# Scores of the slot attention: 56 moving columns in place of 96

## The chip, the cores and the metric

The kernel runs on one core of a Trainium2 chip. The time is the device time of one execution in microseconds (us), from repeated runs; a profile of one execution, taken beside them, gives the trace.

## What is computed

The reference is a two-layer block on 16 sequences (batches) of 56 tokens of width 128, each with a context of 1500 rows. In order: a masked cross attention, a feed-forward with 16 experts, a **slot attention** with a gated recurrent unit (GRU), and a feed-forward with 32 experts and a capacity of 68 tokens each. The change lies in the slot attention:

```python
for _ in range(3):
    sn = rmsnorm(slots, slot_norm_w)
    q_proj = sn @ Wq.T
    scores = jnp.einsum('bkd,bmd->bkm', q_proj, k_proj) * SCALE
    attn = jax.nn.softmax(scores, axis=-2)          # over the 56 slots
    attn = attn / (jnp.sum(attn, axis=-1, keepdims=True) + EPS)
    updates = jnp.einsum('bkm,bmd->bkd', attn, v_proj)
    slots = gru_cell(updates, slots, gru_wih, gru_whh, gru_bih, gru_bhh)
```

The slots are the 56 token rows of a batch, so a batch has 56 query columns against 1500 keys. All matrices are fp32.

## The kernel before

Everything is written by hand: every engine has its own list of instructions in a fixed order, and semaphores (`wait_ge`, `then_inc`) tie them together. No planner moves anything.

**Tiling of the slot attention.** The 1500 keys of a batch are 12 chunks of 125 (`CP`, `CC`). Keys stand twice in SBUF: `keysT` (128 features x 1500, weights of the scores) and `keys` (125 keys x 129 columns per chunk, moving operand of the update, the 129th column for the sum). There is room for 8 batches (`GB`), so the 16 batches run as 2 groups. Two batches make a pair, a group has 4 pairs (`TWO`), and 3 iterations over 4 pairs are 12 **phases** per group, 24 in all. The Python function `phase` of each engine issues one phase; `phases` runs them, partly in hardware loops of four phases.

**Steps.** A phase has four **steps** (`step_of`): half of the key chunks (6, `CH`) of one of its two batches. Each step runs through the engines as follows.
- PE, `scores` (L1586 to L1600): for each of 6 chunks, two matmuls into two column strips of the array (64 and 61 key columns as weights, rows 0 to 63 and 64 to 124 of PSUM). The moving operand is the batch's queries in `qT`. The output goes to bank 2 + 2a + h, at column c*56 for chunk c. Before a step it waits for the queries, the keys and, four steps back, for ACT to have emptied the bank.
- DVE, `maxima` (L1190): the maximum over the 56 slots of each key, read from PSUM (L1197), times the key's norm (L1200).
- ACT, `exponentials` (L850): six exponentials of 56 columns (L859) from PSUM into `A`.
- DVE, `attention` (L1202): sums (L1208) and reciprocals (L1212).
- POOL, `weigh` (L696): the reciprocal times the key's norm (L702), then the shares times it (L704).
- PE, `update` (L1602), for every two steps: 12 matmuls with `A` as weights and `keys` moving (129 columns, L1611).

Steps are issued ahead: in each phase PE issues steps 3, 4, 5 and 6 counted from the phase's first, so the scores run three to six steps before their use. Between them stand the GRU of the pair of the phase before (`gru_start`, `gru_gates`: L1583 on PE, then L866, L867 and L872 on ACT, L1225 to L1242 on DVE) and the projection and queries for a later phase (`slot_proj`, `queries` on PE, L876 on ACT, L687 and L689 on POOL, L1256 and L1260 on DVE). Each engine takes its list in order.

**Loads.** The keys of the second group are loaded by SyncE (L562, L564); each load waits until the update of the last phase that uses the slot has run (L560).

**The padded columns.** A listed fp32 matmul shows as two passes, each with its weight load. In `scores` each matmul moves `WIDE` = 96 columns from `qT`, of which 56 are the batch's queries; the others are those of the second batch, or zeros. `qT` has 40 more columns per pair for it, set to zero by POOL at L671. The last 40 columns of each chunk's output fall on the place of the next chunk, which overwrites them; behind the last chunk they go to columns that nobody reads. `WIDE` serves the last feed-forward too (L1727, L1741), which the change leaves alone.

Of the kernel before, what the change touches and what calls it, by code (L numbers as in the profile page):

```python
# [15 lines left out]
B, S, D, M = 16, 56, 128, 1500  # L16
# [24 lines left out]
TWO = GB // 2  # L41
QS = 2 * S
# [7 lines left out]
WIDE = 96  # L50
# [17 lines left out]
def build_program(nc, t):  # L68

    with ExitStack() as ctx:  # L70
        def sb(name, shape, dt=F32):
            return ctx.enter_context(nc.sbuf_tensor(name, shape, dt))
# [98 lines left out]
        r1 = sb("r1", [128, NT])  # L171
# [13 lines left out]
        work = sb("work", [128, 4 * CC * S + 7 * HALF])  # L185
# [4 lines left out]
        def carve(n, where="region"):  # L190
            tile = {"region": region, "work": work, "early": early, "early_rest": early_rest}[where]
            used[where] += n
            assert used[where] <= tile.shape[1]
            return tile[:, used[where] - n:used[where]]
# [55 lines left out]
        pair_rows = ident[:, :].rearrange("p (i q) -> p i q", i=2)[:, :, 0:S]  # L250
        slots_x = carve(TWO * QS, "work").rearrange("p (a s) -> p a s", a=TWO)

        qT_all = carve(TWO * (QS + WIDE - S), "work")
        qT = qT_all.rearrange("p (a s) -> p a s", a=TWO)
        Un, rt, zt, nt, hn, tmp = (carve(QS, "work") for _ in range(6))
        Pn = carve(128, "work")
# [20 lines left out]
        ps = ctx.enter_context(nc.psum_tensor("ps", [128, 8, 512], F32))  # L277
# [151 lines left out]
        def half(h):  # L429
            return slice(h * HALF, (h + 1) * HALF)  # L430
# [5 lines left out]
        def by_tile(ap):  # L436

            return ap.rearrange("p (b t q) -> p t b q", t=TILES, q=QT)
# [21 lines left out]
        def step_of(p, m):  # L460

            h, i = divmod(m, 2)
            return 2 * p + i, h, i
# [931 lines left out]
        def _(pe):  # L1395
# [19 lines left out]
            for f, (left, right) in enumerate(((wqT, wkT), (wvT, wo))):  # L1415
                for q in range(4):
                    if f:
                        pe.wait_ge(fold_ev, q + 1)
                    r0 = DH * (q % 2)
                    for m in range(4):  # L1420
                        pair = 4 * (q // 2) + m
                        mm = pe.matmul(ps[:, 4 + q, m * 128:(m + 1) * 128], left[r0:r0 + DH, pair, :],
                                       right[r0:r0 + DH, pair, :], start=True, stop=True)
# [5 lines left out]
            for b in range(B):  # L1429
                pe.wait_ge(key_add3, b + 2)  # L1430
                pe.matmul(ps[:B, 3, 0:CC // 4 * 128], key_sel[:, b, :], padd[b % 2][:CP, :],
                          start=(b == 0), stop=(b == B - 1), skip_group_check=True).then_inc(key_sum, 1)
# [8 lines left out]
                if b == 6:  # L1441
                    pe.wait_ge(plan_hot, KB)
                    pe.wait_ge(plan, PLAN_LISTS)
                    for bank, col, items, left in ((4, 0, ITEMS, lambda b: lists_w[:, b, 0:1]),
# [5 lines left out]
                        for blk in range(KB):  # L1450
                            mm = pe.matmul(ps[:rows, bank, col:col + items], left(blk), hot_r[blk][:BT, 0:items],
                                           start=(blk == 0), stop=(blk == KB - 1))
# [4 lines left out]
            for h in range(2):  # L1457
                mm = pe.matmul(ps[:, 5 + h, 0:HALF], ones[:BT, :], keep_d[:BT, half(h)], start=True, stop=True)
# [18 lines left out]
            with pe.Fori(0, (n + 1) // 2) as i:  # L1477
                for k in range(2):
                    j = pe.snap(i * 2 + k)
                    pe.wait_ge(p_exp, j + 1)  # L1480
                    for c in range(KC):
                        mm = pe.transpose(ps[:KP, 2, c * 128:(c + 1) * 128],
                                          P[k][:, c * KP:(c + 1) * KP], ident[:, :])
# [5 lines left out]
                    for c in range(KC):  # L1489
                        mm = pe.matmul(ps[:, 3, 0:128], PT[:KP, c, :], ictx[k][:KP, c, :], start=(c == 0), stop=(c == KC - 1))  # L1490
# [14 lines left out]
            with pe.Fori(0, tiles) as i:  # L1505
                tile = bass.ds(pe.snap(TILES - 1 - i), 1)
                for head in range(H):
                    mm = pe.matmul(ps[:, bass.ds(i, 1), 0:B * QT], MO[:, head, :],
                                   by_tile(tilesT[:, head, 0:T])[:, tile, :, :],
                                   start=(head == 0), stop=(head == H - 1))  # L1510
# [6 lines left out]
            for j in range(NT):  # L1517
                mm = pe.matmul(ps[:, 4, j * E0:(j + 1) * E0], xln[:, j * 128:(j + 1) * 128], gw0[:, :], start=True, stop=True)
# [25 lines left out]
            for j in range(NT):  # L1544
                c = j * 128

                for c0, c1 in ((c, min(c + 128, max(c, HALF))), (max(c, min(HALF, c + 128)), c + 128)):
                    if c1 > c0:
                        mm = pe.matmul(ps[:PARTS, 6 + c0 // HALF, c0 % HALF:c0 % HALF + c1 - c0],
                                       parts[:, j, :], ident_b[:, c0 - c:c1 - c], start=True, stop=True)  # L1550
# [35 lines left out]
            def scores(g, p, v_, m):  # L1586
                s, h, a = step_of(p, m)
                n = v_ * STEPS + m
                pe.wait_ge(q_ok, v_ + 1)
                pe.wait_ge(ld_keys[s], (g + 1) * 48)  # L1590
                if not isinstance(n, int) or n >= 4:
                    pe.wait_ge(a_exp, n - 3)

                for c in range(CH):
                    c0 = (h * CH + c) * CP
                    for r0, r1 in ((0, COL), (COL, CP)):
                        mm = pe.matmul(ps[r0:r1, 2 + 2 * a + h, c * S:c * S + WIDE],  # L1597
                                       keysT[:, s, c0 + r0:c0 + r1],
                                       qT[:, p, a * S:a * S + WIDE], start=True, stop=True)
                mm.then_inc(a_mm, 1)  # L1600

            def update(g, p, v_, h, bank):  # L1602
# [49 lines left out]
            for m in range(LOOK):  # L1652
                scores(0, 0, 0, m)

            def phase(g, c, v_):
                def scores_ahead(m):
                    to = steps_ahead(g, c, m)
                    if to:
                        scores(to[0], to[1], v_ + to[2], to[3])

                scores_ahead(3)
                scores_ahead(4)
                scores_ahead(5)
                if cell_runs(g, c):
                    gru_start(v_ - 1, (c - 1) % TWO)
                update(g, c % TWO, v_, 0, 6 + c % 2)
                if renews(g, c):
                    slot_proj(v_ + 2, (c + 2) % TWO, 6 + (c + 1) % 2)
                scores_ahead(6)
                if cell_runs(g, c):  # L1670
                    gru_gates(v_ - 1)
                update(g, c % TWO, v_, 1, 6 + c % 2)
                if renews(g, c):
                    queries(v_ + 2, 6 + (c + 1) % 2)
# [8 lines left out]
            for j in range(NT):  # L1683
                mm = pe.matmul(ps[:, 0, j * E1:(j + 1) * E1], xln[:, j * 128:(j + 1) * 128], gw1[:, :], start=True, stop=True)
            mm.then_inc(lg1_mm, 1)
            for c in range(4):
                src = (xln, xT)[c // 2]
                j0, j1 = ((0, 4), (4, NT))[c % 2]
                for j in range(j0, j1):
                    mm = pe.transpose(ps[:, 4 + c, (j - j0) * 128:(j - j0 + 1) * 128], src[:, j * 128:(j + 1) * 128], ident[:, :])  # L1690
                mm.then_inc(tok_mm, 1)
            pe.wait_ge(rt1_hot, 1)
            for j in range(NT):
                for i in range(j + 1):
                    mm = pe.matmul(ps[:, 1, j * E1:(j + 1) * E1], before_b[:, :] if i == j else ones_b[:, :],
                                   ohb[:, i, :], start=(i == 0), stop=(i == j))
# [146 lines left out]
```

## Time and profile before

| | |
|---|---|
| runs | 616.84 us median of 3 (612.61 to 617.85) |
| the profiled execution | 618.72 us, span of its trace 616.9 us |
| TensorE (PE) matmul busy | 491.4 us (80%), 6216 instructions |
| VectorE (DVE) busy | 385.0 us (62%) |
| ScalarE (ACT) busy | 323.5 us (52%) |
| GpSimd (POOL) busy | 220.4 us (36%) |
| mean granted TensorE clock | 0.891 of 2.4 GHz |
| scores, L1597 | 2304 listed passes, 106.4 us busy, mean 249 ns of one |
| chain that ended last | PE 55%, DVE 13%, DMA 11%, SyncE's queue 7% of the span |

The slot attention runs from about 262 to 501 us. Busy times of PE overlap (a pass is counted from its issue to its modelled end), so 249 ns is no price of a pass. The clock has two levels, 1.00 (2.4 GHz) and 0.50 (1.2 GHz); values between are means over a stretch. Waits are shown where an engine stood idle and are put down to the work that ended last before it went on.

### The profile page before, as it was taken

The numbers are of one execution on the slowest core, as the hardware profiler recorded it, in microseconds if no ns is written. First come the engines' busy times: TensorE is split into PE (matmuls) and PEld (weight loads), VectorE is DVE, ScalarE is ACT, GpSimd is POOL, SyncE is SP. The second block draws the span as 40 slices with busy tenths as digits, with TensorE's granted clock in tenths as the row PEclk, the third lists the DMA queues.
The fourth block names the chain that finished last, engine by engine and source line by source line (L and its number), as shares of the span: only waits on it lengthen the run. The fifth ranks groups of instructions, "written<-read, shape, count | busy, mean of one in ns | idle before, by whom it ended". The sixth has DMA issues, their size and how long they took to land.

```text
span 616.9 us, 17523 instructions
## 1 busy us (share of the span) xinstructions
PE 491.4 (80%) x6216; PEld 375.7 (61%) x6216; DVE 385.0 (62%) x1149; ACT 323.5 (52%) x959; POOL 220.4 (36%) x414
## 2 busy tenths in 40 slices
PE   3687888887687899699999997889999856039990
PEld 2522224554474454289999996789899734039990
DVE  1569964555635544458989996779899845103332
ACT  3363664344322122378988986678988731023330
POOL 5366852122420000135445453435445400622241
PEclk9797987889986799989999998999999975559996
DMA  8887743343219999800000399910000099130003
GB/s 250 175 201 173 222 150 102 100 112 110 76 28 256 228 205 171 315 3 2 4 3 0 86 247 225 212 37 2 3 0 1 2 387 428 40 95 12 28 29 102
DMA packets 52589, 74.36 MB, mean 121 GB/s; under 512 B 6853, under 2 KB 46198, under 8 KB 51510
## 3 DMA queue, kind: packets, MB, share of 16 engines
q1 hardware_dynamic: 48380, 61.78, 40.9%
q0 software_dynamic: 1424, 7.81, 3.5%
q10 hardware_dynamic: 2730, 4.03, 2.2%
q8 instruction: 36, 0.59, 0.4%
q14 instruction: 19, 0.16, 0.1%
HBM read 69.07 MB, written 4.54 MB: 119 GB/s over the span
## 4 chain that ended last, share of the span: by engine, by line
PE 55%; DVE 13%; DMA 11%; SPq 7%; ACT 4%; issue 4%; POOL 3%; POOLq 1%; ACTq 0%; DVEq 0%
PE ps L1597 12%; PE ps L1611 8%; PE ps L1583 7%; SPq L562 6%; PE ps L1528 4%; PE ps L1727 4%; PE ps L1741 3%; DMA region<-in_wo 3%; DMA work<-in_kv_blk 3%; PE ps L1562 2%; POOL xe_scratch L746 2%; PE ps L1465 2%; DVE sumsq L991 2%; DMA region<-in_ctxT 2%; PE ps L1436 2%
## 5 line engine op out<-in xcount | busy, mean ns | idle before, releaser
L859 ACT ACTIVATE work<-ps,nb,rkey 125x56 f32<-125x56 f32 x576 | 173.3, 467 | 6.5 <-DVE nb L1200 6.3
L1597 PE MATMUL ps<-work,region 128*64 128x96 f32 (+1 forms) x2304 | 106.4, 249 | 4.0 <-issue 2.9
L1597 PEld LDWEIGHTS ps<-work,region 128*64 128x64 f32 (+1 forms) x2304 | 102.3, 138 | 8.2 <-issue 4.8
L1611 PE MATMUL ps<-region,work 125*64 125x129 f32 x1152 | 75.3, 278 | 5.1 <-issue 2.7
L704 POOL TENSOR_TENSOR work<-work,rs 125x336 f32<-125x336 f32 x96 | 71.9, 749 | 7.5
L1611 PEld LDWEIGHTS ps<-region,work 125*64 125x64 f32 x1152 | 65.5, 138 | 8.5 <-POOL work L704 3.7
L702 POOL TENSOR_TENSOR rs<-rs,rkey 125x6 f32<-125x6 f32 x96 | 19.3, 201 | 112.9 <-DVE rs L1212 112.8
L1197 DVE TENSOR_REDUCE ps<-ps 125x6 f32<-125x336 f32 x96 | 48.8, 508 | 6.6 <-PE ps L1597 6.3
L1208 DVE TENSOR_REDUCE sm<-work 125x6 f32<-125x336 f32 x96 | 47.4, 494 | 1.4 <-ACT work L859 1.3
L1583 PE MATMUL ps<-GI,work 112*64 112x112 f32 (+3 forms) x288 | 34.5, 314 | 6.9 <-DVE work L1221 2.5
L631 POOL TENSOR_TENSOR region<-early_w 125x768 f32<-125x768 f32 x16 | 29.1, 1820 | 22.4 <-DMA early_w<-in_ctx 22.0
L1436 PE MATMUL ps<-xln,folded 128*128 128x448 f32 x64 | 29.9, 592 | 6.2 <-ACT region L786 6.2
L771 ACT ACTIVATE region<-early_w 125x1536 f32<-125x1536 f32 x16 | 23.8, 1490 | 18.4 <-DVE sumsq L991 14.7
L991 DVE TENSOR_REDUCE sumsq<-region 125x12 f32<-125x1536 f32 (+1 forms) x16 | 27.7, 1747 | 8.4 <-ACT region L771 8.4
L752 POOL DMA_INDIRECT ys_scratch<-folded,yidx x17 | 16.3, 957 | 44.1 <-ACT folded L930 41.3
L843 ACT ACTIVATE early_w<-ps 128x448 f32<-128x448 f32 (+1 forms) x18 | 9.8, 542 | 42.4 <-PE ps L1528 42.4
L1528 PE MATMUL ps<-xln,early_w 128*128 128x448 f32 x64 | 30.7, 611 | 0.0
L802 ACT ACTIVATE early_w<-m_before,m_minus 128x1 f32 (+1 forms) x22 | 6.5, 294 | 40.6 <-DVE m_minus L1079 40.6
L650 POOL COPY work<-region 128x128 f32 x22 | 6.9, 314 | 57.3 <-DMA work<-in_kv_blk 49.8
L1465 PE MATMUL ps<-work 128*128 128x375 f32 x44 | 22.6, 602 | 4.9 <-POOL work L651 4.8
L1436 PEld LDWEIGHTS ps<-xln,folded 128*128 128x128 f32 x64 | 11.3, 197 | 23.0 <-ACT region L786 14.5
L1173 DVE TENSOR_TENSOR early_w<-early_w,ps 128x448 f32<-128x448 f32 (+1 forms) x18 | 11.1, 619 | 22.7 <-ACT early_w L843 22.7
(298 smaller groups left out, 970.4 us busy)
## 6 DMA issues: line engine op xcount, KB each, us to landing
region<-in_w SPq DMA_DIRECT2D x6, 2048.0 KB, 18.4
region<-in_ctxT SPq DMA_DIRECT2D x16, 750.0 KB
early_w<-in_ctx SPq DMA_DIRECT2D x16, 672.0 KB
region<-in_ctx SPq DMA_DIRECT2D x16, 672.0 KB
work<-in_ctxT_blk SPq DMA_DIRECT2D x22, 187.5 KB
early_w<-in_w POOLq DMA_DIRECT2D x1, 4096.0 KB, 13.7
region<-in_ctx_blk ACTq DMA_DIRECT2D x11, 187.5 KB
early_w<-in_ctx_blk ACTq DMA_DIRECT2D x10, 187.5 KB
```

The costliest lines, as they stand in the source:

```text
L562: sp.dma_start(keys[p0:p1, s, :, 0:128], ctx_b[g * GB + s, p0:p1, :].rearrange("p (c d) -> p c d", c=CC)).then_inc(ld_keys[s], 16)
L704: gp.tensor_tensor(shares_of(p, a, h), shares_of(p, a, h), bcast(rs[:, a, c], S), ALU.mult).then_inc(a_att, 1)
L859: i = act.activation(shares_of(p, a, h)[:, c, :], ps[:CP, 2 + 2 * a + h, c * S:(c + 1) * S], ACT.Exp, bias=nb[:, a, q:q + 1], scale=rkey[: ...
L991: v.tensor_reduce(sumsq[:, bass.ds(b, 1), :], msq[k][:CP, :].rearrange("p (a c d) -> p a c d", a=1, d=D), AX.X, ALU.add).then_inc(key_ss, 1)
L1197: v.tensor_reduce(mx, ps[:CP, 2 + 2 * a + h, 0:CH * S].rearrange("p (c s) -> p c s", s=S), AX.X, ALU.max).then_inc(a_max, 1)
L1208: v.tensor_reduce(sm[:, a, c], shares_of(p, a, h), AX.X, ALU.add).then_inc(a_sum, 1)
L1436: pe.matmul(ps[:, h, 0:HALF], G[:, b, :], xln[:, half(h)], start=True, stop=True).then_inc(qa_mm, 1)
L1465: pe.matmul(ps[:, k, 0:KN], Qk[k], ictxT[k], start=True, stop=False)
L1528: mm = pe.matmul(ps[:p, 2 * (j % 2) + g, 0:HALF], w, xln[:, half(h)], start=True, stop=True)
L1583: mm = pe.matmul(out[r0:r1], w[:, r0:r1], x, start=start, stop=stop, **more)
L1597: mm = pe.matmul(ps[r0:r1, 2 + 2 * a + h, c * S:c * S + WIDE], keysT[:, s, c0 + r0:c0 + r1], qT[:, p, a * S:a * S + WIDE], start=True, sto ...
L1611: mm = pe.matmul(ps[i * COL:(i + 1) * COL, bank, 0:KW], A[:CP, p % 2, i, h, c * S:c * S + COL], keys[:, 2 * p + i, h * CH + c, :], start=( ...
```

## The change

The score matmuls move the 56 columns of their own batch and write just the 56 columns of their chunk. The query tile `qT` shrinks from 152 to 112 columns per pair.

```diff
@@ -250,7 +250,7 @@
-        qT_all = carve(TWO * (QS + WIDE - S), "work")
+        qT_all = carve(TWO * QS, "work")
         qT = qT_all.rearrange("p (a s) -> p a s", a=TWO)
@@ -1594,9 +1594,9 @@
                 for c in range(CH):
                     c0 = (h * CH + c) * CP
                     for r0, r1 in ((0, COL), (COL, CP)):
-                        mm = pe.matmul(ps[r0:r1, 2 + 2 * a + h, c * S:c * S + WIDE],
+                        mm = pe.matmul(ps[r0:r1, 2 + 2 * a + h, c * S:(c + 1) * S],
                                        keysT[:, s, c0 + r0:c0 + r1],
-                                       qT[:, p, a * S:a * S + WIDE], start=True, stop=True)
+                                       qT[:, p, a * S:(a + 1) * S], start=True, stop=True)
                 mm.then_inc(a_mm, 1)
```

## Rows read from the trace of the kernel before

**Rows 1.** The page's chain that ended last, by line, share of the span.
```profile
PE ps L1597 12%; PE ps L1611 8%; PE ps L1583 7%; SPq L562 6%; PE ps L1528 4%; PE ps L1727 4%; PE ps L1741 3%; DMA region<-in_wo 3%; DMA work<-in_kv_blk 3%; PE ps L1562 2%; POOL xe_scratch L746 2%; PE ps L1465 2%; DVE sumsq L991 2%; DMA region<-in_ctxT 2%; PE ps L1436 2%
```

**Rows 2.** Windows: two steady phases; length, busy us per engine, granted clock, DMA.
```profile
294.18:303.07 8.89, 8.89 (x184) 8.39 (x182) 8.18 (x29) 8.06 (x30) 4.49 (x10) 1.00 0.01 3
303.07:311.97 8.90, 8.90 (x186) 8.40 (x183) 8.19 (x29) 8.07 (x30) 4.48 (x10) 1.00 0.01 4
```

**Rows 3.** The chain inside the first of these phases: start, length, instructions.
```profile
294.18 2.97 PE ps L1597 x72
...
297.92 1.45 PE ps L1611 x24
...
299.95 0.99 PE ps L1597 x24
...
301.52 1.33 PE ps L1611 x24
```

**Rows 4.** Waits from 294 to 356 us: us in total, times, longest.
```profile
ACT work L866 <- PE ps L1583: 6.2, 7, 1.2
...
DVE work L1260 <- issue: 0.3, 1, 0.3
PE ps L1597 <- issue: 0.3, 1, 0.3
```

**Rows 5.** Timeline of DVE, first and last row of one phase: start, length, instruction.
```profile
303.39 0.15 DVE L1217 TENSOR_SCALAR zr<-ps 128x1 f32<-128x1 f32 x1
...
312.29 0.15 DVE L1217 TENSOR_SCALAR zr<-ps 128x1 f32<-128x1 f32 x1
```

**Rows 6.** Timelines of DVE, POOL and PE, 307 to 311 us, and DVE's tail.
```profile
307.40 0.74 DVE L1242 SCALAR_TENSOR_TENSOR work<-work 128x112 f32<-128x112 f32 x1
...
307.27 0.75 POOL L704 TENSOR_TENSOR work<-work,rs 125x336 f32<-125x336 f32 x1
...
309.14 0.75 POOL L704 TENSOR_TENSOR work<-work,rs 125x336 f32<-125x336 f32 x1
309.85 0.19 POOL L687 TENSOR_TENSOR ss<-ss,eps_sum 112x1 f32<-112x1 f32 x1
...
310.24 1.50 PE L1611 MATMUL ps<-region,work 125*64 125x129 f32 x24
...
500.51 0.28 DVE L1242 SCALAR_TENSOR_TENSOR work<-work 128x112 f32<-128x112 f32 x1
```

**Rows 7.** Timeline of PE: one moving column, 128 weight columns, at both clocks.
```profile
183.89 1.80 PE L1403 MATMUL ps<-mean_w,ln_tiles 128*128 128x1 f32 x14 [0.57 <-ACT ln_tiles L761]
...
503.62 3.15 PE L1403 MATMUL ps<-mean_w,ln_tiles 128*128 128x1 f32 x14 [0.17 <-ACT ln_tiles L761]
```

**Rows 8.** The chain at the stage's start, and a window of it.
```profile
262.83 3.86 PE ps L1597 x48
...
267.47 4.73 ACT work L859 x16
...
264.00:266.00 2.00, 2.00 (x30) 2.00 (x28) 0.68 (x2) 0.45 (x2) 0.00 (x0) 0.50 0.02 4
```

**Rows 9.** The chain at the end of the key loads, and in the tail.
```profile
395.68 10.75 DMA region<-in_ctxT
...
406.66 1.21 PE ps L1597 x24
...
481.78 0.99 PE ps L1597 x24
```

**Rows 10.** Windows in the thin stretches: length, busy us per engine, granted clock, DMA.
```profile
372.00:376.00 4.00, 1.54 (x32) 1.35 (x29) 2.72 (x11) 0.89 (x5) 2.84 (x8) 1.00 0.94 231
376.00:380.00 4.00, 3.50 (x40) 3.50 (x41) 0.55 (x2) 2.44 (x9) 0.00 (x0) 0.57 1.16 225
...
400.00:404.00 4.00, 2.40 (x48) 2.26 (x46) 2.08 (x9) 3.78 (x14) 1.33 (x3) 1.00 0.72 164
...
492.00:496.00 4.00, 1.71 (x28) 1.44 (x28) 2.29 (x9) 0.99 (x3) 0.10 (x1) 1.00 0.37 90
```

## The prediction

> **What bounds the kernel now.** I started with the chain of waits, which walks back from the last instruction. In the slot attention stage it names TensorE nearly everywhere, and the two matmul groups of the attention lead the whole kernel: L1597 (the scores, the line of the change) with 12% and L1611 with 8% [rows 1]. Next I cut the steady stretch into phases, one pair of batches each. Two neighbouring phases last 8.89 and 8.90 us; PE is marked busy for all of it, at the full granted clock (2.4 GHz), but DVE is busy for 8.18 of 8.89 us and ACT for 8.06 [rows 2]. So PE is the top of the list by a little, and a busy PE is not PE at its peak. The question is which of the three would set the pace if the others were faster.
>
> The chain inside one phase has three score steps in 2.97 us, one more in 0.99 us and two halves of the update in 1.45 and 1.33 us [rows 3]. A step is 24 listed instructions (12 matmuls, each run as two passes), and its two column strips stream side by side: 12 pairs, 82.5 ns each. Against that, the waits between 294 and 356 us, seven phases: DVE waited 0.3 us in all, once, and for issue; ACT waited 6.2 us for PE, 0.9 us a phase; PE itself waited 0.3 us [rows 4]. Then DVE's own order of time: L1217 stands at 303.39 and again at 312.29, 8.90 us later, with 28 other instructions between that follow each other end to start [rows 2, 5]. The missing 0.7 us of the busy share are the gaps of about 35 ns between dependent instructions. The reader is to see two saturated engines: the chain follows PE only because it has to choose one. **DVE is full by itself**, and a DVE that never waits cannot be sped up by an earlier matmul.
>
> One piece of DVE's phase is a stall of another kind: L1242 takes 0.74 us in the phase and 0.28 us in the tail. It starts while POOL's L704 (307.27, 0.75 us) runs and ends with it [rows 6]. That L704 is released by DVE's own L1212, so PE has no part in it.
>
> **The change part by part.** (1) 2304 listed score passes stream 56 columns in place of 96. The stream alone would be 0.99 x 56/96 = 0.58 us a step. But each pass also loads 64 columns of weights. The row nearest to a load-bound pass is L1403, one moving column against 128 weight columns: 14 passes in 1.80 us at 2.4 GHz, with two breaks in it, and 14 in 3.15 us at 1.2 GHz, without [rows 7]. Half of the columns and twice the clock of the second give 3.15/14/4 = 56 ns a pair, 0.68 us a step; the first gives 64 ns, 0.77 us. No row has 64 weight columns under fewer than 96 moving ones, so the bounds are 0.58 and 0.99 us (nothing gained; a loss is excluded, since nothing is added to any pass). I take 0.68, the row without breaks: 0.31 us less a step, 1.24 us less a phase, PE's share 8.89 -> 7.65 us. In the steady phases this lies wholly beside DVE's 8.89 us, so it is worth **0**; its cover is DVE's work, and if DVE were not full, see the first rival. ACT's wait of 0.9 us for the gates shrinks, and ACT, busy 8.06 us, then waits for DVE instead. What is late next is thus DVE, unchanged.
>
> (2) Where DVE is not yet full, or no longer, steps lie on the path. Start: two steps take 3.86 us at 1.2 GHz before ACT's run of L859 at 267.47 [rows 8]. At that clock a load-bound step is 3.15/14/2 x 12 = 1.35 us, so the second step ends 1.2 us earlier; ACT then first needs its six exponentials of step 0 (4.73/16 = 0.30 us each), which leaves 0.8 us of it: -0.8 (between 0 and -1.2). Loop borders: DVE's only wait, 0.3 us, may go: -0.3 (0 to -0.9, there are three such borders on the path). Change of group: the key loads wait for the update of the pair that frees them. PE starts the second half of the update at 310.24 while POOL's weighing that it needs ran from 309.14 to 309.89 [rows 6], so a PE with room starts it up to 0.4 us earlier, and the loads, issued in a row, shift with it: -0.4 (0 to -0.4). All phases under those loads, from about 357 to 406 us, are covered by them: 10.75 us of the chain before 406.43 are the last of these transfers [rows 9]. Restart behind them: one step of 1.21 us and one of 0.99 us before DVE fills again: -0.6 (0 to -0.8). Tail: one step of 0.99 us before the gates [rows 9]: -0.3 (0 to -0.4).
>
> (3) The query tile loses its four pads of 40 columns: a memset on POOL writes 448 columns in place of 608, once, long before it is awaited (0 either way), and tiles behind it in the work region move down. The writes of a step into PSUM no longer overlap by 40 columns; the order of the writes and every wait stays. No instruction, DMA, queue or semaphore is added or moved: 0.
>
> (4) The clock. PE will be idle more. The rows show how it stood so far: between 372 and 376 us PE was busy 1.54 of 4 us at the full clock, and the next 4 us have a mean of 0.57, so nearly all of them ran at 1.2 GHz, with PE busy again; in 400 to 404 us it was busy 2.40 of 4 us and in 492 to 496 us 1.71 of 4 us, both times at the full clock [rows 10]. A steady phase of 7.65 us of work in 8.89 stays far above these. The thin stretches (around 400 us, the tail) get thinner by up to 0.3 us a step. I allow one more stretch at 1.2 GHz like that of 376 us; 3.5 us of PE busy there would be 1.75 at the full clock, partly behind other work: +0.8 (0 to +3.5). [...]
>
> **Sum.** -0.8 -0.3 -0.4 -0.6 -0.3 +0.8 = -1.6 us against the profiled execution, whose time is 618.72 us with a span of 616.9: 617.1. The median of the runs shown is 616.84, 1.9 us below it, so the forecast is 615.2, call it **615 us**, -0.3%. All terms at their ends give -3.7 and +3.5. Runs of this kernel spread over 612.61 to 617.85; about 1% is what a measurement can tell from no change.
>
> **The rivals.** (A) *PE is the bound.* For it: the chain, and PE's 8.89 of 8.89 us. Against it: DVE has no wait that PE could shorten. If DVE's gaps could close, a phase could fall from 8.89 to its busy 8.18 us (PE's 7.65 is below that): 0.7 us in 18 of 24 phases that are not under the key loads, 12.6 us, and with the 1.6 of above 616.8 - 14.2 = **about 602 us**. Half of it would be 609. Chance 0.10.
>
> (B) *The clock stays down* (the other side). At 1.2 GHz a load-bound score step takes 1.35 us, of which the 56 columns stream for seven eighths; such steps might not bring the clock back after the start [rows 8] or behind the key loads, or a phase that waits in the middle might lose it. A phase at 1.2 GHz costs PE 4 x 1.35 + 2 x (8.89 - 3.96) = 15.3 us against 8.89: +6.4 us, so it decides from one phase on that runs cold. For it: the clock fell whenever PE thinned out. Against it: it has risen in every stretch in which PE worked through, with mixed work. With two or three cold phases: 616.8 + 13 to 19, **about 632 us**. Chance 0.15.
>
> (C) *The port moves.* DVE's stalls against POOL (0.46 us of L1242 and some of L1231) depend on who starts first. If POOL's small operations for the slot norm, released over ACT by PE's projection, come at another moment, a phase gains or loses up to 0.5 us, 12 us over 24 phases: **605 or 629 us**. Against it: POOL takes them in a written order behind a weighing that DVE releases, and L687 now starts at 309.85, when that ends [rows 6]. Chance 0.03 on either side.
>
> (D) *A pass has a floor that hides the narrower stream* and PE saves nothing. With DVE full that can't be told in the time: 616 us, within the forecast.
>
> **How the numbers follow.** Forecast with (D) 0.69, (A) 0.10, (B) 0.15, (C) 0.06. Faster by over 1%: 0.10 + 0.03 = 0.13; slower by over 1%: 0.15 + 0.03 = 0.18; within 1%: 0.69. The forecast's own range is 613 to 620, its terms' ends and the spread of the runs. To leave out no more than 2 in 10 it has to reach into the others: 607 takes in the weak forms of (A), 626 those of (B): **607 to 626 us**.
>
> **What would show it.** Right: steady phases still 8.9 us with DVE's instructions end to start; L1597 x24 at 0.6 to 0.8 us in the chain or gone from it; PE busy about 7.7 of 8.9 us; the chain of the stage now runs through DVE; waits of PE for POOL or ACT appear; granted clock 1.00 in all steady phases, mean no lower than 0.88. The start's first L859 run begins near 266.7 us. Wrong: phases under 8.6 us (A), stretches of clock 0.50 inside 270 to 480 us that are new (B), L1242 at another duration than 0.74 us (C), or a step still at 0.99 us (D).

## The result and the profile after

The changed kernel takes **611.54 us** (median of 20 runs, 607.7 to 615.41) against 616.36 us (20 runs, 610.56 to 625.4) for the kernel before in the same sessions: ratio 0.9948, 95% interval 0.9923 to 0.9974. So it is faster by about half a per cent, 3.2 us (1.6 to 4.7). The forecast was 615 us, -0.3%, inside 607 to 626. The profiled execution took 607.94 us with a span of 606.2; the one of before took 618.72. Most of the 10.7 us between the two spans lies ahead of the first score matmul (262.6 us in before, 253.4 in after), where the change touches nothing but a shorter memset and the place of some tiles. The later experiments have that first score at 253.8 to 256.2 us with 56 columns and at 254.3 to 257.5 us with 96, so I take most of this part for the chance of one execution and leave it out in what follows. I compare the stage, from the first score matmul to the end of the last L1248: **238.5 us before, 236.9 us after, -1.6 us** (e7 below, whose code is the same in this stage, takes 237.0).

The page of after, the busy times and the chain (shares by engine, then by line), against 491.4 us of PE and [rows 1]:

```profile
PE 464.3 (77%) x6216; PEld 344.3 (57%) x6216; DVE 386.3 (64%) x1149; ACT 323.7 (53%) x959; POOL 220.6 (36%) x414
...
PE 34%; DVE 33%; issue 9%; POOL 7%; DMA 7%; ACT 6%; POOLq 1%; ACTq 1%; DVEq 1%; SPq 0%
DVE ps L1197 6%; DVE sm L1208 6%; PE ps L1528 4%; PE ps L1727 4%; PE ps L1741 3%; DMA work<-in_kv_blk 3%; PE ps L1611 2%; PE ps L1583 2%; POOL work L704 2%; PE ps L1562 2%; ACT work L859 2%; POOL xe_scratch L746 2%; DVE sumsq L991 2%; PE ps L1408 2%; PE ps L1597 2%
```

L1597 has gone from the top of the list to its end, from 12% to 2%, and DVE's two reductions lead it. 27 us less of PE's busy time bought 1.6 us: the chain of before had named an engine that could be named, not the one that set the pace. Windows of two steady phases of after (length, busy us of PE, its weight loads, DVE, ACT and POOL, granted clock, DMA), against [rows 2]:

```profile
281.60:290.41 8.81, 8.11 (x186) 7.28 (x182) 8.10 (x29) 8.05 (x29) 4.49 (x11) 1.00 0.02 5
290.41:299.22 8.81, 8.11 (x186) 7.29 (x182) 8.11 (x29) 8.06 (x29) 4.49 (x11) 1.00 0.01 3
```

A phase is 8.81 us in place of 8.89, at the full clock; PE now has room, DVE and ACT are as busy as before. The waits of after over seven phases (us in total, times, longest; PEld is TensorE's weight load), against [rows 4]:

```profile
PEld ps L1611 <- POOL work L704: 6.0, 7, 0.9
ACT work L866 <- PE ps L1583: 5.1, 7, 0.9
PE ps L1611 <- POOL work L704: 4.5, 7, 0.6
...
DVE work L1260 <- issue: 0.3, 1, 0.3
PE ps L1597 <- issue: 0.3, 1, 0.3
```

PE waits for POOL's weighing, 0.64 us a phase, where it did not before, and POOL is released by DVE. DVE still shows one wait in seven phases, the same one. The 0.08 us a phase are in its timeline all the same. The end of its `update` and the next maxima, in before and then in after:

```profile
303.77 0.35 DVE L1221 TENSOR_SCALAR work<-ps,zr 128x128 f32<-128x128 f32 x1
304.11 0.52 DVE L1197 TENSOR_REDUCE ps<-ps 125x6 f32<-125x336 f32 x1
```
```profile
301.89 0.35 DVE L1221 TENSOR_SCALAR work<-ps,zr 128x128 f32<-128x128 f32 x1
302.16 0.51 DVE L1197 TENSOR_REDUCE ps<-ps 125x6 f32<-125x336 f32 x1
```

Start to start it is 0.34 us in before and 0.27 us in after. In before, L1197 starts just as L1221 ends and looks unhindered; in after it starts 0.08 us **before** that end, which is what an unhindered pair does here (0.27 us in every phase of after up to the key loads, and once in before, at 441.5 us). So DVE did wait for the scores, once a phase, by less than an idle time shows.

Where the stage's 1.6 us come from, by the starts of L1208 (96 of them, four a phase):

| part of the stage | before | after | difference |
|---|---|---|---|
| first score to the 9th L1208 | 19.36 | 18.41 | -0.95 |
| to the 45th (9 phases) | 82.17 | 80.85 | -1.32 |
| to the 61st (4 phases, key loads) | 46.25 | 48.07 | **+1.82** |
| to the 69th (2 phases, restart) | 18.70 | 17.98 | -0.72 |
| to the 96th | 61.18 | 60.74 | -0.44 |
| tail | 10.88 | 10.88 | 0.00 |

The start as foretold: the chain of after has one run of L859 right behind the first score step, against [rows 8]:

```profile
253.57 1.29 PE ps L1597 x22
...
255.64 7.05 ACT work L859 x24
```

The loss is under the key loads. Waits of PE there, in before (356 to 406 us) and then in after (345 to 396 us):

```profile
PE ps L1583 <- issue: 3.0, 1, 3.0
PE ps L1611 <- issue: 2.7, 2, 1.6
PE ps L1597 <- issue: 2.4, 1, 2.4
```
```profile
PE ps L1611 <- issue: 4.3, 2, 2.3
PE ps L1597 <- issue: 3.0, 1, 3.0
PE ps L1583 <- issue: 2.6, 1, 2.6
```

PE stands for 1.1 to 3.0 us at a time for nothing that the profile shows, four times in each kernel, 8.1 us together in before and 9.9 us in after. The stands alone are thus 1.8 us longer in after. Behind some of them the clock falls too; windows of after at the end of the loads:

```profile
388.00:392.00 4.00, 1.67 (x37) 1.53 (x34) 2.30 (x8) 3.09 (x13) 1.81 (x5) 1.00 0.46 125
392.00:396.00 4.00, 4.00 (x76) 4.00 (x73) 1.93 (x7) 1.50 (x6) 0.00 (x0) 0.57 0.02 4
```

From 392 us on PE works without a gap, mostly at 1.2 GHz, and DVE is busy 1.93 of 4 us: here the chain's engine and the pace are PE again, with no transfer left to blame (DMA share 0.02).

### The profile page after: what moved, and what is told of

The parts are those of the page before. It is cut to its first block, busy times and chain, and to the rows that moved or that the text cites. A ratio compares the mean times of both kernels' runs of the same rounds, so it can differ in the third digit from the quotient of the medians.

```text
span 606.2 us, 17523 instructions
## 1 busy us (share of the span) xinstructions
PE 464.3 (77%) x6216; PEld 344.3 (57%) x6216; DVE 386.3 (64%) x1149; ACT 323.7 (53%) x959; POOL 220.6 (36%) x414
## 4 chain that ended last, share of the span: by engine, by line
PE 34%; DVE 33%; issue 9%; POOL 7%; DMA 7%; ACT 6%; POOLq 1%; ACTq 1%; DVEq 1%; SPq 0%
DVE ps L1197 6%; DVE sm L1208 6%; PE ps L1528 4%; PE ps L1727 4%; PE ps L1741 3%; DMA work<-in_kv_blk 3%; PE ps L1611 2%; PE ps L1583 2%; POOL work L704 2%; PE ps L1562 2%; ACT work L859 2%; POOL xe_scratch L746 2%; DVE sumsq L991 2%; PE ps L1408 2%; PE ps L1597 2%
## 5 line engine op out<-in xcount | busy, mean ns | idle before, releaser
L859 ACT ACTIVATE work<-ps,nb,rkey 125x56 f32<-125x56 f32 x576 | 173.2, 469 | 7.7 <-DVE nb L1200 7.6
L1597 PEld LDWEIGHTS ps<-work,region 128*64 128x64 f32 (+1 forms) x2304 | 79.0, 143 | 9.1 <-issue 5.9
L1597 PE MATMUL ps<-work,region 128*64 128x56 f32 (+1 forms) x2304 | 80.3, 227 | 4.8 <-issue 3.6
L704 POOL TENSOR_TENSOR work<-work,rs 125x336 f32<-125x336 f32 x96 | 71.9, 749 | 7.5
L1197 DVE TENSOR_REDUCE ps<-ps 125x6 f32<-125x336 f32 x96 | 48.6, 506 | 5.5 <-PE ps L1597 5.4
L1208 DVE TENSOR_REDUCE sm<-work 125x6 f32<-125x336 f32 x96 | 47.5, 494 | 2.2 <-ACT work L859 2.2
L1583 PE MATMUL ps<-GI,work 112*64 112x112 f32 (+3 forms) x288 | 37.6, 330 | 8.1 <-DVE work L1221 2.8
L1528 PE MATMUL ps<-xln,early_w 128*128 128x448 f32 x64 | 28.9, 580 | 0.0
L1583 PEld LDWEIGHTS ps<-GI,work 128*64 128x64 f32 (+2 forms) x288 | 17.6, 141 | 19.2 <-DVE work L1256 8.8
L1465 PE MATMUL ps<-work 128*128 128x375 f32 x44 | 20.5, 550 | 5.9 <-POOL work L651 5.9
```

Of the source, the lines that this page charges most:

```text
L704: gp.tensor_tensor(shares_of(p, a, h), shares_of(p, a, h), bcast(rs[:, a, c], S), ALU.mult).then_inc(a_att, 1)
L859: i = act.activation(shares_of(p, a, h)[:, c, :], ps[:CP, 2 + 2 * a + h, c * S:(c + 1) * S], ACT.Exp, bias=nb[:, a, q:q + 1], scale=rkey[: ...
L1197: v.tensor_reduce(mx, ps[:CP, 2 + 2 * a + h, 0:CH * S].rearrange("p (c s) -> p c s", s=S), AX.X, ALU.max).then_inc(a_max, 1)
L1208: v.tensor_reduce(sm[:, a, c], shares_of(p, a, h), AX.X, ALU.add).then_inc(a_sum, 1)
L1528: mm = pe.matmul(ps[:p, 2 * (j % 2) + g, 0:HALF], w, xln[:, half(h)], start=True, stop=True)
L1583: mm = pe.matmul(out[r0:r1], w[:, r0:r1], x, start=start, stop=stop, **more)
```

## The experiments

**Is it DVE or PE?** Theory D: DVE sets the steady phase, PE close behind. Theory P: PE sets it. The first four runs cross the width of the stream with a relief of DVE.

**e1_stream80**, the kernel before with a width of its own for the scores (`SW`), in the tile and both slices:

```diff
-                        mm = pe.matmul(ps[r0:r1, 2 + 2 * a + h, c * S:c * S + WIDE],
+                        mm = pe.matmul(ps[r0:r1, 2 + 2 * a + h, c * S:c * S + SW],     # SW = 80
...
-                                       qT[:, p, a * S:a * S + WIDE], start=True, stop=True)
+                                       qT[:, p, a * S:a * S + SW], start=True, stop=True)
```

Expected: 

> Scores stream 80 columns, between the 96 of before and the 56 of the change. Theory D (DVE's own work sets a steady phase; PE at 96 columns was just behind it): a step takes 12 x (160/2.4 + 2.5 ns) = 0.83 us (0.99 before, 0.69 after), but the phase is already down to the 8.81 us of after, and the time is within 2 us of after, about 613. Theory P (PE sets the phase, as the chain of before said): the phase follows the step, 8.89 - 4 x 0.16 = 8.25 us, some 12 us less in all, 605.

Measured: ratio 0.9948 (0.9914 to 0.9982), the same as the change's; steady phase 8.81 us; pairs of passes start 69 ns apart (83 in before). The last 24 columns, from 80 down to 56, bring nothing. The flat part reaches up to 80 columns at least, as theory D says.

**e2_stream112**, the same with `SW = 112`.

Expected: 

> Scores stream 112 columns. A step takes 12 x (224/2.4 + 2.5 ns) = 1.15 us, 0.64 us more PE a phase than at 96. Theory D with PE just behind DVE at 96: PE now sets the phase, 9.4 to 9.55 us, 0.5 to 0.65 us more in some 18 phases, 9 to 12 us more than before: about 627. Had PE had real slack at 96 (0.3 us, what DVE's order of time seemed to say), the phase would be 9.25 us or less and the time 622 or less. Theory P gives 9.53 us, as theory D does.

Measured: ratio 1.0080 (1.0037 to 1.0123), 623.36 us; steady phase 9.23 us. Now DVE waits for the scores in every phase; waits of e2_stream112, 282 to 343 us:

```profile
ACT work L867 <- PE ps L1584: 7.3, 6, 1.4
DVE ps L1198 <- PE ps L1598: 1.3, 7, 0.3
```

A step takes 1.15 us in place of 0.99 (its pairs start 96 ns apart), so PE has 4 x 0.16 = 0.64 us more in a phase, and 9.23 - 0.64 = 8.59 us was its work at 96 columns. PE did have 0.3 us of room in the kernel before; that is the second of the cases in the expectation, and the first, which I held for likelier, was wrong.

**e3_half_max_96**, DVE's maxima over half of the slots, in the kernel before:

```diff
-                v.tensor_reduce(mx, ps[:CP, 2 + 2 * a + h, 0:CH * S].rearrange("p (c s) -> p c s", s=S),
+                v.tensor_reduce(mx, ps[:CP, 2 + 2 * a + h, 0:CH * S].rearrange("p (c s) -> p c s", s=S)[:, :, 0:S // 2],
```

Expected: 

> The kernel before, with DVE's maxima taken over the first 28 of the 56 slots only (the softmax is then shifted by another value; that part of the computation is changed). It takes about 0.25 us off each of the four L1197 of a phase, 1.0 us of DVE's work. Theory D: at 96 columns PE is next in line at once (8.6 to 8.9 us of work), so the phase falls by 0.1 to 0.3 us and the time by 2 to 5 us, to about 613. If DVE alone set the phase with PE well behind, it would fall by 0.8 us (ACT's 8.06 us is the next floor) and the time by 14.

Measured: ratio 0.9883 (0.9838 to 0.9929); phases of 8.50 to 8.76 us, mostly 8.60; L1197 0.34 us in place of 0.51. So a relief of DVE alone shortens the phase with PE's work as it was, which theory P does not allow. The 8.60 us fit the 8.59 us of PE that e2 gave, and PE is busy 59.91 of 60 us. But the relief is smaller than the edit: L1231, another instruction with two inputs, now runs beside POOL's L704 and takes 0.76 us on the mean in place of 0.38. The timeline of e3_half_max_96:

```profile
295.98 0.75 POOL L704 TENSOR_TENSOR work<-work,rs 125x336 f32<-125x336 f32 x1
296.09 0.77 DVE L1231 SCALAR_TENSOR_TENSOR work<-work 128x112 f32<-128x112 f32 x1
```

DVE's own list is therefore 8.81 - 0.70 + 0.37 = 8.5 us, only 0.1 us under the phase. PE's floor of 8.59 us rests on e2, and e3 agrees with it without proving it.

**e4_half_max_56**, the same edit in the changed kernel.

Expected: 

> The changed kernel with the same relief of DVE (maxima over the first 28 slots only, so that part of the computation is changed). Theory D: PE now has 7.7 us of work in a phase, so DVE's relief counts until ACT's 8.06 us: phase 8.1 to 8.3 us in place of 8.81, some 18 phases, 9 to 12 us less than after: about 601. Theory P (PE had been the bound and the change was eaten by something else, a clock or a queue): relief of DVE is worth nothing, 611.5.

Measured: ratio to before 0.9819 (0.9768 to 0.9871), 606.11 us; phases of 8.20 to 8.45 us. ACT is now the fullest. Windows of e3_half_max_96 and e4_half_max_56 over the same 60 us (columns as above):

```profile
282.00:342.00 60.00, 59.91 (x1250) 58.34 (x1248) 54.62 (x195) 55.75 (x202) 31.48 (x70) 1.00 0.01 2
```
```profile
282.00:342.00 60.00, 56.42 (x1298) 52.29 (x1296) 54.15 (x203) 58.10 (x210) 34.42 (x73) 1.00 0.14 33
```

With the scores as they are in after, the relief of DVE is worth 8 us of the whole time (0.9819 against the change's 0.9948): theory P said none, theory D 9 to 12 us; the phase stops above ACT's 8.06 us. Between e3 and e4 the narrower stream is worth 0.15 to 0.4 us a phase, against 0.08 with DVE as it is. The direction is theory D's, but the size is not the stream's alone: L1231 takes 0.32 us on the mean in e4 against 0.76 in e3.

**Could DVE be relieved without leaving anything out?** L1242 takes 0.74 us beside POOL's L704 and 0.28 us alone [rows 6]. **e5_port_96** and **e6_port_56** issue it one step later, `last` being the held-back instruction:

```diff
                     else:
-                        gru_slots_new(v_ - 2, old, slots_x[:, old, :]).then_inc(sl_ok, 1)
+                        last = gru_slots_new(v_ - 2, old, slots_x[:, old, :])
...
                 sums_ahead(3)
+                if cell_ends(g, c) and not leaves(c):
+                    last().then_inc(sl_ok, 1)
```

Expected: 

> The kernel before, with one DVE instruction (L1242, the new slots of the GRU) issued one step later, behind the sums of step 3, so that it no longer stands against POOL's weighing of step 2. Nothing is left out. Theory D with the port: its 0.74 us become 0.28, DVE's list shrinks by up to 0.36 us a phase, but PE at 96 columns has 8.6 us of work, so the phase goes from 8.89 to 8.6 us; some 18 phases, 5 us less than before. If L1242 is long for another reason than POOL's instruction, or meets the next one, the phase stays at 8.9.

Expected: 

> The changed kernel with the same DVE instruction one step later. Theory D with the port: phase 8.81 - 0.36 = 8.45 us (PE 7.7, ACT 8.06), some 18 phases, 6 to 7 us less than after, about 605 where after gives 611.5; here narrowing the scores is worth 0.15 us a phase more than in the pair without the move. Rival: the stall moves to another instruction with two inputs (L1231), and half of it comes back: phase 8.65.

Measured: e5 ratio 1.0087 (1.0046 to 1.0128), phase 9.32 us; e6 ratio 0.9951 (0.9904 to 0.9999), phase 9.03 us, 0.22 us **more** than without the move. Both expectations failed, and not in the part on the port. The timeline of DVE and the waits of e6_port_56, then the chain of e5_port_96 behind the moved instruction:

```profile
299.23 0.28 DVE L1240 SCALAR_TENSOR_TENSOR work<-work 128x112 f32<-128x112 f32 x1
299.95 0.50 DVE L1208 TENSOR_REDUCE sm<-work 125x6 f32<-125x336 f32 x1 [0.45 <-ACT work L859]
300.49 0.19 DVE L1212 RECIPROCAL rs<-sm 125x6 f32<-125x6 f32 x1
300.59 0.23 DVE L1241 SCALAR_TENSOR_TENSOR work<-work 128x112 f32<-128x112 f32 x1
```
```profile
PEld ps L1584 <- DVE work L1241: 5.0, 7, 0.7
PE ps L1584 <- DVE work L1241: 3.3, 7, 0.5
DVE sm L1208 <- ACT work L859: 2.6, 6, 0.5
POOL ss L687 <- ACT work L876: 1.8, 7, 0.3
```
```profile
303.61 0.65 PE ps L1584 x3
304.26 0.99 PE ps L1598 x24
305.25 0.60 PE ps L1584 x11
```

The moved instruction (L1241 there) does fall from 0.74 to 0.23 us: the stall is POOL's doing. The Trainium skill says the same ("SBUF — State Buffer", Who interferes with whom: a VectorE instruction with two SBUF inputs and a GpSimd instruction that reads SBUF exclude each other). But it writes the new slots, and PE's projection waits for them, 0.5 us a phase now. Behind the projection stand, in PE's fixed order, one score step and the gates; ACT's L866 waits for the gates (0.9 us in e6, 1.2 us in e5) and has the exponentials behind it, and DVE's third sums wait for those, 0.45 us, ahead of the moved instruction. A loop over DVE, PE and ACT has become the bound. In e5 one score step of 0.99 us stands in this loop, and at 56 columns it is 0.3 us shorter; the phase goes from 9.32 to 9.03 us, 0.29 us, nearly four times what the narrower stream is worth in the kernel as it is.

**The middle under the key loads.** **e9_no_reload_96** and **e10_no_reload_56** cut the second group's loads to little, with all waits in place:

```diff
+                    cn, mn = (1, 16) if g else (CC, M)
                     for p0, p1 in ((0, 112), (112, CP)):
-                        sp.dma_start(keys[p0:p1, s, :, 0:128],
+                        sp.dma_start(keys[p0:p1, s, 0:cn, 0:128],
...
-                    sp.dma_start(keysT[:, s, :], t["ctxT"][g * GB + s]).then_inc(ld_keys[s], 16)
+                    sp.dma_start(keysT[:, s, 0:mn], t["ctxT"][g * GB + s][:, 0:mn]).then_inc(ld_keys[s], 16)
```

Expected: 

> The kernel before, with the key loads of the second group cut to one chunk of keys and 16 columns of keysT (the second group then attends to keys of the first: that part of the computation is left out). The waits and the order stay. Theory M (the middle of the stage, 4 phases in which they cost 40 to 46 us, is slow because of the transfers: PE's instructions come late, 2 to 3 us at a time, and the clock falls): the 4 phases go to about 9.3 us each and the time falls by some 12 us, to about 604. Rival: the recurrence of the slots over the group's border costs it, transfers or not; then less than 3 us are gained.

Expected: 

> The changed kernel with the same loads cut. If the change's loss in the middle (it spends 48.1 us between the same two DVE instructions where before spends 46.2) comes from the transfers and the cold clock, it is gone here, and this kernel beats the one above by what the change gives outside: 0.09 us in each steady phase, 0.8 to 1.7 us at the start, 0.3 in the tail, 3 to 4 us together. If the narrower scores cost something by themselves, the difference stays at 1.6 us or under.

Measured: e9 ratio 0.9835 (0.9745 to 0.9925), 604.00 us; e10 0.9813 (0.9704 to 0.9922), 602.31 us. The whole times are too coarse to tell the two apart; the profiles are not. The four phases take 36.5 and 36.1 us in place of 46.2 and 48.1, the stage 229.0 and 225.5 us: **3.6 us for the change without the loads, 1.6 us with them**. PE's waits for issue are gone, and the clock stays up. Windows over 40 us in the loads, before and then e9_no_reload_96:

```profile
350.00:390.00 40.00, 35.35 (x679) 33.43 (x675) 32.46 (x112) 30.37 (x110) 19.12 (x48) 0.96 1.12 238
```
```profile
340.00:380.00 40.00, 39.09 (x808) 37.21 (x806) 37.51 (x131) 35.86 (x130) 20.02 (x50) 1.00 0.08 17
```

So the transfers cost the stage 10 to 12 us, by holding PE up for issue and by a lower clock. The change loses its 1.8 us there only in the presence of the loads; without them it gains 0.4 us in the same four phases.

**e12_stream64**, `SW = 64`, to see the price of a pass and to have the middle once more.

Expected: 

> Scores stream 64 columns, as many as each pass loads of weights. If a pass is bound by its weight load (56 ns a pair, the price taken in the prediction), a step takes the 0.69 us of the 56 columns, though 14% more is streamed; if the stream of 56 still counts (0.58 us and a fixed part), a step takes 0.75 to 0.79 us. The steady phase is 8.81 us either way, and the time that of after, a ratio of 0.995. The four phases under the key loads, 46.2 us in before and 48.1 us in after, come at 47.5 or more if the thinner stream lengthens them, and anywhere from 45 to 48 if that was chance.

Measured: ratio 0.9956 (0.9903 to 1.0009). Three steps in a row take 2.31 us against 2.30 at 56 columns, so a step is the same 0.7 us: the stream of 56 columns no longer counts. What counts is the weight load: at both widths the strip with 64 weight columns starts its passes 58 ns apart and the one with 61 columns 56 ns (medians from 282 to 342 us; 82 ns in both strips at 96 moving columns), and L1403, with 128 weight columns, starts them 112 ns apart at the same clock. Steady phase 8.81 us. The four phases under the loads take 45.5 us, which by the bound in the expectation speaks for chance. Put beside the other profiles, with the time at 1.2 GHz and PE's stands for issue in this part of the stage (us, in the order of the profiles named):

| scores | profiles | four phases | of it at 1.2 GHz | stands for issue |
|---|---|---|---|---|
| 56 columns | after, e4, e7, e11 | 48.1, 48.1, 48.1, 48.2 | 10.2 each | 10.0, 13.0, 11.2, 11.9 |
| 56, L1242 later | e6, e8 | 46.6, 46.7 | 10.2, 9.8 | 10.4, 8.0 |
| 64 | e12 | 45.5 | 6.8 | 8.3 |
| 80 | e1 | 45.4 | 3.4 | 8.1 |
| 96 | before, e3, e5 | 46.2, 46.9, 45.1 | 3.4, 3.4, 0 | 8.0, 9.2, 8.8 |
| 112 | e2 | 47.9 | 6.8 | 6.9 |

At 56 columns PE spent some 10 us here at half clock in all six profiles, at 96 columns 3.4 or none in three. But the stands differ as well: five of those six have 10 us or more of them, the three at 96 columns 8.0 to 9.2. That the thinner stream makes the clock fall more often under the loads is a pattern of twelve single profiles, not a measured cause. Whether the change's 1.8 us there come from the clock or from the longer stands was not tested: no run held the clock up at 56 columns with the loads in place.

**Where the narrower stream does pay.** The last feed-forward pads its 68 columns to 96 in the same manner, and there PE is full while DVE is not. A window of before in that stage (columns as above):

```profile
560.00:580.00 20.00, 20.00 (x432) 18.50 (x428) 7.51 (x17) 7.47 (x19) 5.75 (x6) 1.00 0.07 22
```

**e7_experts_68** is the changed kernel with

```diff
-                        mm = pe.matmul(ps[r0:r0 + COL, HIDDEN_BANK[e % DEEP], c * CAP:c * CAP + WIDE],
+                        mm = pe.matmul(ps[r0:r0 + COL, HIDDEN_BANK[e % DEEP], c * CAP:(c + 1) * CAP],
...
-                                       xeT[:, e * CAP:e * CAP + WIDE], start=True, stop=True)
+                                       xeT[:, e * CAP:(e + 1) * CAP], start=True, stop=True)
```

and the same in `result`.

Expected: 

> The changed kernel, and in the last feed-forward the matmuls L1727 and L1741 stream the 68 columns of their expert in place of 96. There PE is busy all the time and DVE and ACT under 40%, so PE is the bound. Pairs of passes at 68 columns: 136/2.4 + 2.5 = 59 ns against 82.5; 64 groups of 8 pairs, 0.66 -> 0.47 us: 12 us less than after, about 600, if nothing else comes up; 8 us if the chain over ACT and DVE per expert shows. Rival (clock): the thinner stream loses the full clock or comes to it later; each 3 us at half clock cost 1.5 us, and with several the gain is gone: 611 or more.

Measured: **599.48 us, ratio 0.9758 (0.9681 to 0.9835)**, 1.9% below the change. The chain of after and then of e7_experts_68 in that stage:

```profile
549.31 0.66 PE ps L1727 x16
549.97 0.66 PE ps L1741 x16
```
```profile
547.23 0.47 PE ps L1727 x16
547.71 0.47 PE ps L1741 x16
```

0.19 us for each of 64 groups, 12 us, all of it on the path. From 550 to 570 us the clock stays at 1.00. The same kind of edit is worth 12 us here and 1.6 us in the slot attention, because the engine that it relieves here is the full one.

**e8_all** is e7 with the move of e6. Expected: 

> All three together: scores of 56 columns, L1242 one step later, experts of 68 columns. If they are independent: 6 to 7 us and 12 us less than after, about 593, 4% less than before. If the clock rival holds in the last stage, about 605.

Measured: 599.67 us, ratio 0.9750 (0.9672 to 0.9827): the experts' gain and nothing of the move, as e6 lets one expect by now.

**e11_experts_half_max** is e7 with the edit of e4. Expected: 

> Scores of 56 columns, experts of 68 columns, and DVE's maxima over the first 28 slots only (the softmax is shifted by another value). Independent terms: 11.7 us of the experts and some 8 us of the maxima less than after: about 593 where before gives 616, ratio 0.963.

Measured: 591.08 us, ratio 0.9607 (0.9529 to 0.9686). Within the interval the terms add up (0.963 was expected). The maximum over half of the slots leaves the softmax unchanged on paper but guards less against overflow, so e7 is the version that I would keep.

## Why the prediction was right, and where it was not

- **DVE is full by itself**: right. e1, e3 and e4 show it, and the chain's 12% for L1597 was no measure of what is to be had. But the worth of a steady phase was put at 0; it was **0.08 us**, 1.4 us in some 17 phases. The failing step is the reading of DVE's order of time, in which the instructions "follow each other end to start": DVE waited for the scores within the overlap of two instructions, where neither the waits nor an end-to-start reading shows it. It would have been seen by holding each pair of instructions against its shortest distance in the trace. The same test shows that the missing 0.7 us of DVE's busy share are not only gaps of about 35 ns: half of it are three pauses of 0.12 us a phase ahead of L1212, alike in both kernels, where the fourth L1212 follows after 0.03 us. No run shows what they wait for, so DVE's 8.81 us are its list with these pauses in it.
- **The price of a step**, 0.68 us by the weight-load row [rows 7]: right, 0.69 in the chain of after; and bound by the weight load, as e12 shows. PE's own 8.89 -> 7.65 us was off at both ends: its work was 8.59 us at 96 columns (e2), so about 7.4 at 56.
- **Start** -0.8: -0.95. The clock rose 4.2 us after the first score in before and 2.4 us after it in after, but that is not what made the start shorter: in e8, with 56 columns, it rose at 4.3 us, and the start took the same 18.46 us as in e7. **Loop borders** -0.3: the two phases that hold one outside the loads went from 9.48 and 9.55 to 9.29 and 9.54 us, -0.04 in all beside the steady 0.08 of each. **Restart** -0.6: -0.72, of which 0.16 are steady phases; without the loads it is -0.17 (e9, e10). **Tail** -0.3: 0.00; why the shorter step brings nothing there was not tested.
- **Change of group** -0.4, "All phases under those loads" being "covered by them": wrong. This step failed. The chain of before named the last transfer for 10.75 us [rows 9], and I took the loads as a floor under all four phases. In after the loads end by 392 us and the stage is no further ahead; what costs the time is PE, held up for issue and then at 1.2 GHz, both set off by the transfers (e9, e10). Most of it are the stands: in e5 the clock never fell there, and its four phases still took 45.1 us, against 37.3 for four of its steady ones.
- **Clock** +0.8 (0 to +3.5): the sign and the place fit, the size does not, and the cause is open. The middle lost 1.8 us, with three stretches at 1.2 GHz for one, but also with stands for issue that were 1.8 us longer. In the steady phases the clock never fell, as said.
- The **sum** was -1.6 us and the stage measured -1.6 us. That is partly luck: 1.4 us of steady phases that I had left out paid for a loss under the loads that I had made too small, and for gains in the group's change and tail that did not come. The measured -3.2 us (1.6 to 4.7) holds the 1.6 at its edge; where the rest lies, if it is real, no single profile tells.
- Rival (A), PE as the bound, gave 602 us for phases of 8.2 us: refuted, save for the 0.08. Rival (B), the clock: more time at 1.2 GHz under the loads, none in the steady phases. In the tail it fell in seven of the other profiles (3.6 to 5.8 us), at 96 columns too (e9). Rival (C): e5 and e6 show the port's stall to be real and tied to POOL; the change leaves L1242 at 0.74 us, but in e3 the stall of L1231 did grow, by 0.37 us. Rival (D): refuted, steps fell from 0.99 to 0.69 us.

## What to carry to other kernels

When the chain of waits runs through one engine and another shows no waits either, the chain may have picked the wrong one: make a list of each engine's own work per period (here PE 8.59, DVE 8.81, ACT 8.06 us) and expect of a relief only the distance to the next. A padded stream costs only where its engine is the longest of that list: 40 columns were worth 0.5% in one stage, 28 columns 1.9% in another. And an instruction that looks too long because of a neighbour may still stand where it must; before it is moved, ask who waits for what it writes.

## What the runs showed of the hardware

- Two column strips of the array with 64 weight columns each, fp32: pairs of passes start about 57 ns apart at both 56 and 64 moving columns, and 69, 83 and 96 ns at 80, 96 and 112, at 2.4 GHz. At 56 and 64 the distance goes by the weight columns: 58 ns with 64 and 56 ns with 61.
- During transfers of about 240 GB/s PE waited for issue four times in before and four times in after, 1.1 to 3.0 us each, in code that has no such waits with the transfers cut (e9, e10: none in the same 55 us).
- A two-input DVE instruction of 0.23 to 0.28 us took 0.74 to 0.77 us when it met a POOL instruction of 0.75 us (L1242 in before, L1231 in e3).
